# A gated attention and feed-forward block on one core: a new order of the rotation of q, and softmax totals by ones matmuls

## What is computed

```python
q = apply_rope((query @ Wq).reshape(b, t, h, d))
k = apply_rope((key @ Wk).reshape(b, t, kv_h, d))
v = (value @ Wv).reshape(b, t, kv_h, d)
...
def apply_rope(x):
    return x * jnp.cos(phase) + rotate_half(x) * jnp.sin(phase)
...
logits = MAX_ATTN_VAL * jnp.tanh(logits * ATTN_MULT / MAX_ATTN_VAL)
weights = jax.nn.softmax(jnp.where(m, logits, -1e+30), axis=-1)
attn = jnp.einsum('bkgtT,bTkd->btkgd', weights, v)
return attn.reshape(b, t, h * d) @ Wo
...
x = x + jnp.tanh(g_xattn[0]) * attention(_layernorm(x), ctx_4096, ctx_4096, mask)
x = x + jnp.tanh(g_ffn[0]) * ffn(_layernorm(x))
```

## Time and profile before

| | |
|---|---|
| median of 3 runs | 865.17 us (864.29 to 866.2) |
| the profiled execution's own time | 864.27 us |
| its span in the profile | 862.5 us |
| busy: TensorE, weight loads | 774.4 us, 622.0 us |
| busy: VectorE, ScalarE, GpSimd | 641.0, 423.7, 602.7 us |

### The profile page before, as it was taken

One profiled execution on the slowest core, in us unless ns is written; L12 is line 12 of the kernel. 1 busy time (PEld: TensorE's weight loads), 2 busy tenths in 40 slices (PEclk: granted clock), 3 DMA queues, 4 the chain that ended last, 5 costly groups with the idle time before them and its releaser, 6 DMA issues.

```text
span 862.5 us, 11913 instructions
## 1 busy us (share of the span) xinstructions
PE 774.4 (90%) x3650; PEld 622.0 (72%) x3650; DVE 641.0 (74%) x1168; ACT 423.7 (49%) x823; POOL 602.7 (70%) x437
## 2 busy tenths in 40 slices
PE   4757999999999999999999999999767779999998
PEld 3645777777777777777777777777655557888786
DVE  6338887888888788788878878877776668778531
ACT  2355555555555555555555555554444335555420
POOL 4567787788788778878878887879855446666510
PEclk9878999999999999999999999999887979999999
DMA  8401000300200020020002002110020024443010
GB/s 295 158 0 51 0 25 1 98 1 25 98 1 26 1 98 1 25 98 1 25 1 98 1 25 87 37 44 1 0 59 1 0 61 110 105 101 75 1 62 36
DMA packets 57137, 41.70 MB, mean 48 GB/s; under 512 B 22938, under 2 KB 44442, under 8 KB 57082
## 3 DMA queue, kind: packets, MB, share of 16 engines
q1 hardware_dynamic: 57082, 41.03, 16.2%
HBM read 38.90 MB, written 2.11 MB: 48 GB/s over the span
## 4 chain that ended last, share of the span: by engine, by line
POOL 51%; PE 25%; issue 15%; DVE 6%; ACT 1%; DMA 1%; POOLq 0%; SPq 0%; ACTq 0%; DVEq 0%
POOL aT_lo L559 10%; POOL q_rot L477 9%; POOL q_sin L472 9%; POOL probs L543 8%; POOL wo_lo L463 6%; POOL wq_lo L454 5%; PE bank_q L1146 2%; POOL wkv_lo L459 2%; PE bank_q L1147 2%; PE ps_o L52 2%; PE ps_o L54 2%; PE ps_o L53 2%; PE ps_s L52 1%; PE ps_s L53 1%; PE bank_kv L52 1%
## 5 line engine op out<-in xcount | busy, mean ns | idle before, releaser
L472 POOL TENSOR_TENSOR q_sin<-q_sin,q_tab 128x512 f32<-128x512 f32 x64 | 82.9, 1295 | 112.7 <-ACT q_sin L634 112.7
L52 PE MATMUL bank_q<-xT_hi,wq_hi 128*128 128x512 f32 x256 | 110.0, 430 | 6.2 <-ACT q_sin L634 4.8
L633 ACT COPY q_sin<-bank_q 64x512 f32<-64x512 f32 x64 | 37.3, 583 | 149.7 <-DVE q_cos L847 149.7
L52 PE MATMUL ps_o<-wo_hi,aT_hi 128*128 128x512 f32 x256 | 105.3, 411 | 2.3 <-POOL aT_lo L559 1.6
L54 PE MATMUL bank_q<-xT_hi,wq_lo 128*128 128x512 f32 x256 | 104.4, 408 | 0.0
L53 PE MATMUL bank_q<-xT_lo,wq_hi 128*128 128x512 f32 x256 | 104.1, 407 | 0.0
L559 POOL TENSOR_TENSOR aT_lo<-attn,aT_hi 128x512 fp32r<-128x512 f32 x64 | 101.5, 1586 | 2.4 <-ACT aT_hi L727 2.3
L54 PE MATMUL ps_o<-wo_hi,aT_lo 128*128 128x512 f32 x256 | 102.7, 401 | 0.0
L53 PE MATMUL ps_o<-wo_lo,aT_hi 128*128 128x512 f32 x256 | 102.5, 400 | 0.0
L477 POOL TENSOR_TENSOR q_rot<-q_cos,q_sin 128x512 f32<-128x512 f32 x64 | 83.1, 1299 | 5.0
L997 DVE TENSOR_TENSOR p_lo<-probs,p_hi 128x512 fp32r<-128x512 f32 x54 | 84.2, 1559 | 1.6 <-ACT p_hi L694 1.6
(11 more groups left out here) (231 smaller groups left out, 2256.0 us busy)
## 6 DMA issues: line engine op xcount, KB each, us to landing
wo_raw<-in_Wo SPq DMA_DIRECT2D x8, 1024.0 KB, 5.4
wq_raw<-in_Wq SPq DMA_DIRECT2D x7, 1024.0 KB, 5.6
packed<-in_gate_q SPq DMA_DIRECT2D x40, 64.0 KB, 2.3
packed<-in_up_q SPq DMA_DIRECT2D x40, 64.0 KB, 2.3
packed<-in_down_q SPq DMA_DIRECT2D x10, 256.0 KB, 3.4
acc<-in_x SPq DMA_DIRECT2D x8, 256.0 KB, 5.9
wkv_raw<-in_Wk SPq DMA_DIRECT2D x8, 256.0 KB, 2.8
wkv_raw<-in_Wv SPq DMA_DIRECT2D x8, 256.0 KB, 3.2
```

The lines of the kernel that those rows point to most:

```text
L52: nc.tensor.matmul(out, w_hi, m_hi, start=first, stop=False)
L472: nc.gpsimd.tensor_tensor(q_sin[:], q_sin[:], q_tab[:, 1, :].unsqueeze(1).to_broadcast([P, HALF, T]), ALU.mult).then_inc(q_sined, 1)
```

## The change

Three things. *Order of the prologue*: the loads of sequences 2 and 3 go ahead of Wq; the variances are inverted four at a time; four banks instead of two take the transposed sequences; `make_q(0)` comes directly behind the first four; in slot 0 k's rotation and v go ahead of the q job on VectorE and ScalarE. *Rotation of q*: ScalarE turns the halves as soon as q is done, VectorE multiplies in place in the bank behind that, GpSimd keeps only the product with the sines, and the sum is VectorE's (`add_q`), from bank and `q_sin`; `cos_q` moves behind the rotation of k, `add_q` behind `attn`. The banks come free with the sum (`q_roped`) and no longer with the turning. *Totals*: a matrix of ones replaces `fold`; two matmuls of 512 columns with p_hi and p_lo give every partition all totals, VectorE transposes the bank in blocks, inverts one column in 32, and spreads and multiplies as before; transpose and sum of `probs` are gone.

```diff
@@ SP
                 load_x(1)
+                load_x(2)
+                load_x(3)
                 for i in range(2):
                     ks = slice(2 * i, 2 * i + 2)
                     sp.dma_start(wq_raw[0][:, ks, :], wq_v[:, ks, 0:GC]).then_inc(ld_wq0[i], 16)
-                load_x(2)
-                load_x(3)
@@ GpSimd
+                nc.gpsimd.memset(ones[:].bitcast(F32), 1.0).then_inc(ones_done, 1)
...
+                def invert_std(half):
+                    bs = slice(half * HALF, (half + 1) * HALF)
+                    pool.wait_ge(var_done, half + 1)
+                    nc.gpsimd.tensor_tensor(rstd[:, bs, :], rstd[:, bs, :], minus_half[:].unsqueeze(1).to_broadcast([P, HALF, 1]),
+                                            ALU.pow).then_inc(rstd_done, 1)
...
                     nc.gpsimd.tensor_tensor(q_sin[:], q_sin[:], q_tab[:, 1, :].unsqueeze(1).to_broadcast([P, HALF, T]),
                                             ALU.mult).then_inc(q_sined, 1)
-                    pool.wait_ge(q_sined, n + 1)
-                    pool.wait_ge(q_cosed, n + 1)
-                    wait(pool, qk_split, n - h - AHEAD)
-                    nc.gpsimd.tensor_tensor(q_rot[:, half, h, :, :], q_cos[:], q_sin[:], ALU.add).then_inc(q_roped, 1)
@@ ScalarE
                 def turn_q(n):
 
-                    act.wait_ge(q_cosed, n + 1)
+                    act.wait_ge(q_done, n + 1)
                     wait(act, q_roped, n)
...
-                    if has_q_job(s):
+                    if 0 < s and has_q_job(s):
                         turn_q(s + AHEAD)
                     if runs(s):
                         act.wait_ge(kv_done, s + 1)
                         wait(act, pv_done, s - 3)
                         nc.scalar.copy(v_hi[:, s % 4, :], kv_bank(s)[:, 1, :]).then_inc(v_rounded, 1)
+                    if s == 0:
+                        turn_q(AHEAD)
@@ VectorE
                 def cos_q(n):
 
-                    dve.wait_ge(q_done, n + 1)
-                    wait(dve, q_roped, n)
-                    nc.vector.tensor_tensor(q_cos[:], q_banks[n % 2], q_tab[:, 0, :].unsqueeze(1).to_broadcast([P, HALF, T]),
+                    dve.wait_ge(q_turned, n + 1)
+                    nc.vector.tensor_tensor(q_banks[n % 2], q_banks[n % 2], q_tab[:, 0, :].unsqueeze(1).to_broadcast([P, HALF, T]),
                                             ALU.mult).then_inc(q_cosed, 1)
+
+                def add_q(n):
+
+                    g, half, h = q_job(n)
+                    dve.wait_ge(q_cosed, n + 1)
+                    dve.wait_ge(q_sined, n + 1)
+                    nc.vector.tensor_tensor(q_rot[:, half, h, :, :], q_banks[n % 2], q_sin[:], ALU.add).then_inc(q_roped, 1)
...
-                    if runs(s - 2):
-                        dve.wait_ge(masked, s - 1)
-                        wait(dve, norm_done, s - 2)
-                        nc.vector.transpose(r_tot[:], probs[:, s % 2, :]).then_inc(p_turned, 1)
-                        dve.wait_ge(p_turned, s - 1)
-                        wait(dve, tot_done, s - 2)
-                        nc.vector.reduce_sum(partial[:], r_tot[:].rearrange("p (c e) -> p c e", e=32), AX_X).then_inc(p_summed, 1)
-                    if has_q_job(s):
-                        cos_q(s + AHEAD)
...
+                    if has_q_job(s):
+                        cos_q(s + AHEAD)
...
                         wait(dve, norm_done, s - 2)
-                        nc.vector.reciprocal(r_small[:], ps_tot[:, 0:GC // 32]).then_inc(inverted, 1)
+                        nc.vector.transpose(r_tot[:], ps_tot[:]).then_inc(tot_turned, 1)
+                        dve.wait_ge(tot_turned, s - 1)
+                        nc.vector.reciprocal(r_small[:], r_tot[:].rearrange("p (c e) -> p c e", e=32)[:, :, 0]).then_inc(inverted, 1)
...
                         nc.vector.tensor_tensor(attn[:], ps_pv[:], r_tot[:], ALU.mult).then_inc(norm_done, 1)
+                    if has_q_job(s):
+                        add_q(s + AHEAD)
@@ TensorE
                 def prep(b):
 
                     pe.wait_ge(xn_done, b + 1)
-                    wait(pe, x_lo, b - 1)
+                    wait(pe, x_lo, b - 3)
...
-                    wait(pe, q_turned, n - 1)
+                    wait(pe, q_roped, n - 1)
...
-                prep(0)
-                prep(1)
+                for b in range(HALF):
+                    prep(b)
+                make_q(0)
                 pe.wait_ge(mask_step, 6)
                 nc.tensor.transpose(ps_s[:, T:2 * T], live_rows[:], ident[:])
                 nc.tensor.transpose(ps_s[:, 0:T], keep[:], ident[:]).then_inc(keep_T, 1)
-                prep(2)
-                prep(3)
-                for n in range(AHEAD):
-                    make_q(n)
-                    prep(AHEAD + n)
+                prep(4)
+                prep(5)
+                make_q(1)
+                prep(6)
+                make_q(2)
+                prep(7)
+                make_q(3)
...
-                        pe.wait_ge(p_summed, s - 1)
-                        nc.tensor.matmul(ps_tot[:, 0:GC // 32], fold[:], partial[:], start=True, stop=True).then_inc(tot_done, 1)
+                        nc.tensor.matmul(ps_tot[:], ones[:], p_hi[:], start=True, stop=False)
+                        nc.tensor.matmul(ps_tot[:], ones[:], p_lo[:], start=False, stop=True).then_inc(tot_done, 1)
```

More of the change, by code:

```diff
@@ L128, in flamingo_block @@
         cT_hi = sb("cT_hi", [P, B, KT, T], F32R)
-        q_cos = sb("q_cos", [P, HALF, T], F32)
+        q_spare = sb("q_spare", [P, HALF, T], F32)
         q_sin = sb("q_sin", [P, HALF, T], F32)
@@ L160, in flamingo_block @@
         dead = sb("dead", [P, 1], F32)
-        fold = sb("fold", [P, P], F32)
-        partial = sb("partial", [P, GC // 32], F32)
+        ones = sb("ones", [P, P], F32R)
         r_tot = sb("r_tot", [P, GC], F32)
@@ L212, in flamingo_block @@
         ps_g = [bank_q[:], bank_q2[:]]
-        x_banks = [ps_o[:], ps_pv[:]]
+        x_banks = [ps_o[:], ps_pv[:], ps_x[:], ps_tot[:]]
         ps_u = [bank_kv[:], ps_s[:]]
@@ L464, in split_w, with apply_mask, sin_q @@
                                                 wo_hi[par][:, part, :].bitcast(F32), ALU.subtract).then_inc(wo_split, 1)
-                def rope(n):
-                    g, half, h = q_job(n)
+                def apply_mask(s):
+                    pool.wait_ge(exp_done, s + 1)
+                    pr = probs[:, s % 2, :].rearrange("p (h t) -> p h t", h=HG)
+                    nc.gpsimd.tensor_tensor(pr, pr, keepT[:].unsqueeze(1).to_broadcast([P, HG, T]),
+                                            ALU.mult).then_inc(masked, 1)
+                def sin_q(n):
                     pool.wait_ge(q_turned, n + 1)
@@ L634, in turn_q @@
                     nc.scalar.copy(q_sin[D // 2:D], q_banks[n % 2][0:D // 2]).then_inc(q_turned, 1)
-                for b in range(4):
+                round_w("wq", 0, 0)
+                for b in range(3):
                     prep_x(b)
-                    round_w("wq", 0, b)
+                    round_w("wq", 0, b + 1)
+                prep_x(3)
                 round_w("wkv", 0, 0)
-                prep_x(4)
                 round_w("wkv", 0, 1)
                 prep_ctx(0)
+                prep_x(4)
                 prep_x(5)
@@ L701, in cap_and_exp @@
                     wait(act, p_split, s - 1)
-                    wait(act, p_turned, s - 1)
                     nc.scalar.activation(probs[:, s % 2, :], capped[:], ACT.Exp,
@@ L815, in _, with norm_moments @@
             def _(dve):
-                def norm_moments(b):
-                    dve.wait_ge(ld_x[b], 16)
-                    nc.vector.bn_stats(stats[:, b, :], acc[:, b, :]).then_inc(stats_done, 1)
-                    dve.wait_ge(stats_done, b + 1)
-                    nc.vector.bn_aggr(moments[:, b, :], stats[:, b, :]).then_inc(moments_done, 1)
-                    dve.wait_ge(moments_done, b + 1)
-                    nc.vector.tensor_scalar(rstd[:, b, :], moments[:, b, 1:2], EPS, None, ALU.add).then_inc(var_done, 1)
+                def norm_moments(half):
+                    for b in range(half * HALF, (half + 1) * HALF):
+                        dve.wait_ge(ld_x[b], 16)
+                        nc.vector.bn_stats(stats[:, b, :], acc[:, b, :]).then_inc(stats_done, 1)
+                        dve.wait_ge(stats_done, b + 1)
+                        nc.vector.bn_aggr(moments[:, b, :], stats[:, b, :]).then_inc(moments_done, 1)
+                    bs = slice(half * HALF, (half + 1) * HALF)
+                    dve.wait_ge(moments_done, (half + 1) * HALF)
+                    nc.vector.tensor_scalar(rstd[:, bs, :], moments[:, bs, 1:2], EPS, None, ALU.add).then_inc(var_done, 1)
                 def norm_apply(b):
-                    dve.wait_ge(rstd_done, b + 1)
+                    dve.wait_ge(rstd_done, b // HALF + 1)
                     wait(dve, x_T, b - 1)
@@ L878, in _ @@
```

(5 more changed lines are left out.)

72 lines of the change are left out of this document (22 added, 50 removed).

## The result

The changed kernel takes 811.80 us (median of 4 runs, 810.77 to 812.63) against 864.73 of the kernel before in the same runs (863.96 to 866.2): ratio 0.9385, 95% interval 0.9368 to 0.9403. The forecast was 822, 811 to 838. The profiled execution took 812.22 us, its span is 810.4. The forecast gain was 43.6 us; in the spans it is 52.1. So the result lies 0.8 us inside the forecast's range, at its fast end.

The account below looks back on a forecast made before the run. A ring through VectorE and ScalarE was taken to set 9.39 us a slot. Gains 9.7 + 4.1 + 23.5 + 0.3 + 6 = 43.6 took 864.27 to 820.7, the median 0.9 higher: 821.6; range 811 to 838.

Parts of the forecast that it names:

- Steady slots: Slots 4 to 56: TensorE's floor sets 8.95 us a slot instead of 9.39, saving 23.5 us over 53 slots.
- the hole: TensorE's only gap in a steady slot, 0.61 us ahead of the total's matmul, ended by VectorE's partial sums.
- one ring, through VectorE: Steady slots: VectorE's work through cos, ScalarE's two halves and v_hi, then VectorE again, said to set 9.39 us.
- Tail: Slots 60 to 66: without transpose and sum TensorE's waits at the total shrink; gain 6 us (3 to 9).
- Prologue: Start to slot 1: first q-matmul near 15.5 us, slot 1 from about 43.3; gain 9.7 us (7.5 to 11.3).
- Slots 1 to 3: Slots 1 and 2 become 7.4 and 7.1 us, gaining 3.9; slot 3 gains 0.2; together 4.1 (2 to 6).
- Slots 57 to 59: Two matmuls cost 0.24 us where no hole was, slot 57 gains 0.7; together a gain of 0.3 us.
- A: Rival, steady slots: a wait replaces the hole, VectorE's ring is 9.1 to 9.5 us; about 838 us; 14%.
- B: Rival: prologue and tail give 8 us instead of 20, through half clock and late DMA or GpSimd; 834 us; 8%.
- C: Rival: more gain, the 0.47 us of the ones matmuls hidden or the tail better; 808 us; 3%.
- D: Rival: TensorE without its hole is granted 1.2 GHz for some of the steady stretch; at 20%, 917 us; 2%.
- E: Rival: the ones matmuls run in four passes, 1.4 us more a slot, 10.35; 896 us; 2%.

Follow-up runs that it names:

- run with filled waits: The kernel before with twelve identity transposes on TensorE ahead of the total's matmul in slots 60 to 64; 861.02 us, ratio 0.9948.
- run with three more operations: The changed kernel with three more block transposes out of ps_tot on VectorE in slots 2 to 55, results unread; 822.05 us, ratio 0.9503.
- unpack_zeros early: The changed kernel with the three steps of unpack_zeros moved from VectorE's slot 2 into the prologue; 807.39 us, ratio 0.9343.

## Why the prediction was right, and where it was not

**The number.** 811.80 us lies in the range of 811 to 838, by 0.8 us, and outside the 813 to 830 that the forecast called its own. Five of the six terms miss by 2.1 us or less and nearly cancel; the tail alone is 8.7 us over. That the sum held is owed to the mechanism of the steady slots; that the range held is in part luck, since it was made wide for slower cases and the miss went the other way.

**Steady slots (23.5 forecast, 25.6 measured).** Right in its mechanism: the hole goes, TensorE is the bound, turning no longer waits for cos. The floor of 8.95 was 0.04 high, which over 53 slots is the 2.1 us; the idle time ahead of v_lo was 1.15 by forecast and is 1.26. The prices taken for what the trace didn't show held: transpose out of PSUM 0.70, add_q 0.68 (0.60 by starts), the ones matmul 0.23 by starts. On the last the trace and the Trainium skill differ ("TensorE: Matmul & The Clock Gate", Back-to-back issue gap, 131 ns sustained for 512 columns): the rows decide, 0.23 by starts and 0.20 when one is taken out.

Not seen: how the three parts depend on each other. The prediction had one ring, through VectorE, behind the 9.39 us. With transpose and sum taken out of that ring and all else as before, the slot is still 9.29, so a second ring stood 0.10 us behind the first. Steady slots, all measured (the old order with the sum on VectorE was not run):

| order | totals | sum on | slot, us |
|---|---|---|---|
| old | old | GpSimd | 9.39 |
| old | new | GpSimd | 9.29 |
| new | old | GpSimd | 9.10 |
| new | new | GpSimd | 8.92 |
| new | new | VectorE | 8.91 |
| new | old | VectorE | 8.75 |

The prediction costed the whole change at once and so could not see that, given the new order and the sum on VectorE, the small matmul is the cheaper one for the steady slots.

**Tail (6 forecast, 14.7 measured; its own bounds were 3 to 9).** This term carries nearly the whole miss. The step went over waits only, "1.5 to 3 us in three slots and less in two", and the waits did give 7.5. What it left out is the clock. The prediction has "from 100 us on it has the full clock" from a row of 400 to 500 us; in the tail of the kernel before it was 0.83, and 0.74 to 0.85 in slots 60 to 62. So the sum counted a wait by its length alone, and not the matmuls at half clock behind it. The run with filled waits shows the cause, at 3.4 us of the 7.2; that the other 3.8 are the same cause follows from the busy time of the same matmuls only, and no run of its own shows it. The sign of error that the prediction gave, a wait ahead of ps_tot, is absent in the steady slots and present twice in the tail (1.4 and 1.1 us).

**Prologue (9.7 forecast, 8.2 measured).** The step "the pow at 7.7 to 8.3, and the chain apply, transpose, round, rest at 1.2 us a sequence, I get 15.5" failed: the pow ran from 8.52 to 9.55, the two first xn beside GpSimd's weight split took 1.93 us and the fourth 1.51, and the first q-matmul came at 18.16. That cost 2.7 us at its start. q(0) had half clock, as forecast; the jobs behind it ran at full clock (1.00 from 26 us on), and slot 1 came at 44.84 against a forecast 43.3. With the grouping undone the q-matmul is at 15.04 and slot 1 at 41.05.

**Slots 1 to 3 (4.1 forecast, 4.15 measured).** That these agree is luck: the first two gained 4.7 and not 3.9, and slot 3 lost 0.55 and did not gain 0.2. **Slots 57 to 59** lost 0.5 instead of gaining 0.3: slot 57 is 10.11 us (9.66 before), with a wait of 0.93 us for kT_lo that no run looked into.

**The rivals.** A did not happen, since VectorE had 1.5 us to spare; the run with three more operations, past that reserve, gives 9.07 a slot with qT_lo at 1.40, which is close to A's case (9.1 to 9.5, qT_lo at 1.7). B, half clock and late GpSimd in prologue and tail: in the tail it went the other way. C, "the tail better", is what moved the result from 822 towards 808, and 3% was too little for it; its other half, the ones matmuls hidden, did not happen. D did not happen: the clock is 1.00 with TensorE busy for all of the 100 us. E: the ones matmuls run as the p@v ones.

## What to carry to other kernels

Count a wait of TensorE for its own length and, where the granted clock of the stretch is below 1.00, for the matmuls behind it too. Read that clock in every stretch that the change touches: in the steady slots here a hole of 0.61 us in each left it at 1.00, in the tail waits of up to 4.5 us went with 0.74 to 0.85. When one engine is said to have a reserve, see which of its operations are stretched by a neighbour and what moved work would start beside. Price the parts of a change one by one: here the cheapest form of the totals in the steady slots and in the tail are different ones, and the kernel with both (and unpack_zeros early) takes 799.30 us, against 807.39 with the new totals and unpack_zeros early.
